# A transformer layer on one core: the last two gate projections together, the last up projection between the first two pairs of score matmuls

## The reference

```
xn   = layernorm(x)
q, k, v = bitnet_linear(xn, q_weight), ...   # sign of the weights, a scale for each output
scores  = q @ k.T / sqrt(16)                 # 32 heads of 16; 8 key and value heads, each for 4 query heads
attn = softmax(scores) @ v
hidden = silu(xn @ gate_w.T) * (xn @ up_w.T) # 1792 wide, ternary weights with a scale
out  = x + bitnet_linear(attn, o_weight) + hidden @ down_w.T
```

## Time and profile before

| | us |
|---|---|
| median of 3 runs | 501.98 |
| the profiled execution | 501.71 |
| its span | 500.0 |
| PE busy | 480.1 |
| DVE busy | 415.7 |
| ACT busy | 348.1 |
| last unit F27: first matmul | 148.45 |
| first score matmul | 152.01 |

### The profile page before, as it was taken

How to read it: one execution, slowest core, us unless ns; L and a number is a source line. 1 busy time by engine, 2 the same in 40 slices (tenths; PEclk the granted TensorE clock), 3 DMA queues, 4 the chain that set the end, 5 groups by cost and what they waited for, 6 DMA issues and landing times.

```text
span 500.0 us, 10314 instructions
## 1 busy us (share of the span) xinstructions
PE 480.1 (96%) x4171; PEld 163.6 (33%) x4171; DVE 415.7 (83%) x487; ACT 348.1 (70%) x640; POOL 101.7 (20%) x154
## 2 busy tenths in 40 slices
PE   1899999999998999999999999999999999999996
PEld 0564444433332222222222222222222233333442
DVE  7879868676777999999999999999999955223986
ACT  1943543352228999999999999999999978774000
POOL 4212334534424011011011011001101213241021
PEclk9999999999998999999999999999999999999999
DMA  8853783642103812212212312222221133453321
GB/s 263 266 109 84 165 163 41 182 93 24 22 0 40 152 25 42 64 25 43 64 24 44 65 39 47 43 55 34 42 64 25 15 108 94 102 156 86 105 83 45
DMA packets 64424, 39.28 MB, mean 79 GB/s; under 512 B 39729, under 2 KB 53937, under 8 KB 64377
## 3 DMA queue, kind: packets, MB, share of 16 engines
q1 hardware_dynamic: 55352, 27.59, 22.6%
q0 software_dynamic: 8304, 10.95, 11.8%
q10 hardware_dynamic: 720, 0.08, 0.1%
HBM read 33.37 MB, written 10.48 MB: 88 GB/s over the span
## 4 chain that ended last, share of the span: by engine, by line
PE 93%; DVE 3%; ACT 2%; DMA 1%; issue 1%; SPq 0%; ACTq 0%; DVEq 0%
PE ps L1309 28%; PE ps L1144 19%; PE ps L1247 14%; PE ps L1153 11%; PE ps L1217 5%; PE ps L1204 5%; PE ps L1125 4%; PE ps L1339 3%; PE ps L1278 2%; ACT room L718 2%; DMA hlo<-x 1%; DVE stats L777 1%; DVE room L799 1%; PE ps L1117 1%; DVE room L804 0%
## 5 line engine op out<-in xcount | busy, mean ns | idle before, releaser
L853 DVE TENSOR_REDUCE nmx<-ps 128x1 f32<-128x1024 f32 x248 | 283.2, 1216 | 13.4 <-PE ps L1153 13.2
L718 ACT ACTIVATE room<-ps 128x512 f32<-128x512 f32 x512 | 271.1, 598 | 20.5 <-PE ps L1278 11.5
L1309 PE MATMUL ps<-room,vcur 128*32 128x256 f32 (+1 forms) x1880 | 159.8, 412 | 0.3 <-ACT room L718 0.3
L1153 PE MATMUL ps<-kA,qst 48*128 48x512 f16 x496 | 139.3, 384 | 0.0
L1247 PE MATMUL ps<-qst,kB 50*128 50x512 f16 x432 | 134.8, 384 | 1.3 <-ACT room L718 1.3
L1144 PE MATMUL ps<-room,wf 128*128 128x512 f16 x448 | 100.6, 379 | 0.0
L1309 PEld LDWEIGHTS ps<-room,vcur 128*32 128x32 f32 x1880 | 37.2, 108 | 95.0 <-issue 52.1
L699 ACT ACTIVATE room<-ps,gsc 128x512 f32<-128x512 f32 x28 | 19.2, 686 | 62.4 <-PE ps L1144 62.4
L1144 PEld LDWEIGHTS ps<-room,wf 128*128 128x128 f16 x448 | 42.4, 98 | 55.1 <-issue 7.2
L1247 PEld LDWEIGHTS ps<-qst,kB 50*128 50x128 f16 x432 | 28.3, 93 | 97.0 <-ACT room L718 84.6
L562 POOL TENSOR_SCALAR mxs<-mxs 16x128 f32<-16x128 f32 x16 | 8.3, 520 | 214.8 <-DMA mxs<-m_scratch 214.6
(11 more groups left out here) (137 smaller groups left out, 316.9 us busy)
## 6 DMA issues: line engine op xcount, KB each, us to landing
qst<-q_scratch SPq DMA_DIRECT2D x32, 192.0 KB, 3.6
o_scratch<-osb SPq DMA_DIRECT2D x16, 256.0 KB, 2.5
q_scratch<-parts SPq DMA_DIRECT2D x12, 256.0 KB
hlo<-x SPq DMA_DIRECT2D x8, 256.0 KB, 5.3
parts<-x POOLq DMA_DIRECT2D x8, 256.0 KB, 3.7
wf<-gate POOLq DMA_DIRECT2D x14, 128.0 KB, 3.8
wf<-up POOLq DMA_DIRECT2D x14, 128.0 KB, 5.9
wd<-down POOLq DMA_DIRECT2D x1, 1792.0 KB, 13.9
```

The costliest lines, as they stand in the source:

```text
L718: nc.scalar.activation(probs[:, s % 2, r, :], ps[:, bank_of(step, i), :], ACT.Exp, scale=gam_reg[par][r]).then_inc(scores_free, 1)
L853: nc.vector.tensor_reduce(nmx[:, hf, idx:idx + 1], bank_pair(idx % 2), AX.X, ALU.max, negate=True).then_inc(rows_free, 1)
L1153: return nc.tensor.matmul(ps[:, 2 * (idx % 2) + b, :], qst[low:low + KROWS, par, hf, head, qt * P:(qt + 1) * P], kA[low:low + KROWS, par, ...
L1309: mm = nc.tensor.matmul(ps[32 * r:32 * r + 32, value_bank(step_ // TT), of], vcur[:, par, key_tile(r, j), :], probs[:, s % 2, r, of], star ...
```

## The change

Three edits at the passage. On PE, G27 follows G26 at once, then A30 and A31, then U26; U27 is issued in the middle of the first step, behind score 1. On ACT, the rounding of F26 goes behind the first two exponentials, and the wait for U27 stands before the third. The first two exponentials (heads 0 and 2, `EARLY`) are written into the weight buffers 2 and 3 of `wf`, whose last readers are U23 and the units before it, and `times_values` reads them there. `dve_order` and `act_order` are unchanged.

```diff
-                "A17 F20 ... A28 A29 F26 A30 A31 F27 ")
+                "A17 F20 ... A28 A29 G26 G27 A30 A31 U26 ")
...
+    EARLY = ROUND[:REP // 2]
...
+        early_probs = wf[:, :, :, :].rearrange("p a z n -> p (a z n)").bitcast(F32)[:, 2 * HALF:].rearrange("p (r n) -> p r n", r=2)
...
+        def probs_of(step, r):
+
+            if step == 0 and r in EARLY:
+                return early_probs[:, EARLY.index(r), :]
+            return probs[:, step % 2, r, :]
...
-                    if n >= 1:
+                    if 1 <= n < FU - 1:
                         hidden_high(n - 1)
...
+            exps(0, 0, False, range(REP // 2))
+            hidden_high(FU - 2)
             act.wait_ge(up_ready, FU)
-            exps(0, 0, False)
+            exps(0, 0, False, range(REP // 2, REP))
             hidden_high(FU - 1)
...
-                    if opening and i == 0:
+                    if s == 0 and i == 0:
                         pe.wait_ge(gt_ready, FU)
+                    if s == 0 and i == 2:
+                        pe.wait_ge(h_ready, FU - 1)
...
-            pe.wait_ge(h_ready, FU - 1)
             pe.wait_ge(kones_ready, 2)
-            scores(0, 0, opening=True)
+            scores(0, 0, range(REP // 2))
+            feed_forward(FU - 1, 1)
+            scores(0, 0, range(REP // 2, REP))
```

More of the change, by code:

```diff
@@ L60, in layer_kernel @@
                 "F8 A3 A4 F9 A5 F10 F11 F12 A6 A7 F13 F14 A8 A9 F15 A10 A11 F16 A12 A13 F17 A14 A15 F18 A16 S1 F19 "
-                "A17 F20 A18 A19 F21 A20 A21 F22 A22 A23 F23 A24 A25 F24 A26 A27 F25 A28 A29 F26 A30 A31 F27 ")
+                "A17 F20 A18 A19 F21 A20 A21 F22 A22 A23 F23 A24 A25 F24 A26 A27 F25 A28 A29 G26 G27 A30 A31 U26 ")
     dve_order = ("M0 M1 J0 M2 J1 M3 H0 M4 R0 M5 N0 N1 M6 M7 L0 H1 N2 R1 N3 N4 L1 N5 L2 N6 N7 L3 L4 L5 L6 L7 J2 S0 Z0 "
@@ L79, in layer_kernel @@
     assert pe_order.index(("F", SPLIT_AT)) > pe_order.index(("A", UNITS - 1))
-    assert [n for kind, n in pe_order if kind in "FU"] == list(range(FU))
+    assert [n for kind, n in pe_order if kind in "FU"] == list(range(FU - 1))
     assert dve_order.index(("A", SUM_AT - 1)) < dve_order.index(("S", 1)) < dve_order.index(("A", SUM_AT))
@@ L707, in load_scale, with exps @@
                 act.reg_load(gam_reg[par][r], gam_words[0:1, bass.ds(g * REP + r, 1)])
-            def exps(gp, s, last):
+            def exps(gp, s, last, entries=range(REP)):
                 gp_, par, hf, j = at(gp, s)
@@ L715, in exps @@
                 act.wait_ge(probs_free, step + 1)
-                for i, r in enumerate(ROUND):
+                for i in entries:
+                    r = ROUND[i]
                     act.wait_ge(scores_ready, step * REP + i + 1)
-                    nc.scalar.activation(probs[:, s % 2, r, :], ps[:, bank_of(step, i), :], ACT.Exp,
+                    nc.scalar.activation(probs_of(step, r), ps[:, bank_of(step, i), :], ACT.Exp,
                                          scale=gam_reg[par][r]).then_inc(scores_free, 1)
@@ L1220, in down_proj, with scores @@
                     mm.then_inc(down_ready, 1)
-            def scores(gp, s, opening=False):
+            def scores(gp, s, entries=range(REP)):
                 gp_, par, hf, j = at(gp, s)
                 block_ = gp * 4 + s // TT
-                if j == 0:
+                if j == 0 and 0 in entries:
                     pe.wait_ge(q_loaded[par][hf], 32 * (gp_ + 1))
@@ L1258, in scores @@
                             half_rows(1 - par, hf, idx, half).then_inc(rows_ready, 1)
-                    if i % 2 == 1 and not opening:
+                    if i % 2 == 1 and s > 0:
                         times_values(gp, s - 1, i // 2, 2)
@@ L1309, in times_values @@
                     mm = nc.tensor.matmul(ps[32 * r:32 * r + 32, value_bank(step_ // TT), of], vcur[:, par, key_tile(r, j), :],
-                                          probs[:, s % 2, r, of], start=(j == 0 and part == 0),
+                                          probs_of(step_, r)[:, of], start=(j == 0 and part == 0),
                                           stop=(j == TT - 1 and part == cut - 1))
```

## The result

| | before | changed |
|---|---|---|
| median of 22 runs, us | 502.2 | 504.9 |
| lowest and highest, us | 500.27, 505.42 | 503.19, 507.44 |
| profiled execution's span, us | 500.0 | 501.5 |

The ratio is 1.0057, 95% interval 1.0042 to 1.0072: the change makes the kernel 2.1 to 3.6 us slower. In a second comparison (12 and 33 runs, medians 505.42 and 502.65) it is 1.0062, 1.0031 to 1.0092. Three executions that lie far above the others of their kernel (766 us in e5, 1140 us in e10, 510 us in e6) count in no ratio.

What follows compares the result with a forecast made beforehand. The prediction took DVE's row maxima from R5 on to bound the kernel. It added 0.78 us for R5's later reduction and 1.3 for the halved clock to 501.71, giving 503.8 us, range 501.9 to 504.9 (8 in 10).

Steps and rivals of the forecast that it cites:

- What bounds the kernel: Attention from R5 on: DVE's row maxima set the pace, 1.1315 us each; moving R5's reduction moves the end equally.
- G26, G27, ACT: Passage before attention: G27 waits 0.10 us, score 0 issued at 150.36, Exp table loaded before it.
- ACT's old wait: PE's 1.28 us idle for the late Exp table load and exponentials; forecast to go, worth nothing by itself.
- The new wait: PE before R0: idle 1.72 us until DVE reduces A30, which stands behind F26's product; R0 issued at 152.47.
- Rival "faster": Wait at R0 does not bind, A30 being reduced before score 0 is issued: -1.33, 500.4 us; chance 0.07.
- slow stretch: PE at half clock after idle time; before, 156.2 to 159.5 us, costing DVE 1.50 us; one forecast after the change.
- The price of the wait and the order without the clock: R5's reduction starts at 161.23 against 160.45 if DVE runs R0 to R5 without a hole: +0.78 us.
- The clock: Idle time before U27 or R2 can halve PE's clock; price taken as 1.3 us, between 0 and 1.73.
- Same wait, clock stays at 1.00: Rival: PE waits at R0 but no slow stretch follows, 502.5 us; chance 0.24.
- The base: Whole kernel before: the profiled execution's 501.71 us, without adding the 0.27 by which the median of runs lay above.
- the two terms of the sum: Added to the kernel before: +0.78 us for R5's later reduction and +1.3 us for the halved clock.
- Two slow stretches in one run: Rival: half clock once in U27 and once behind R2, 4.0 us more, 505.7 us; chance 0.10.

Runs made afterwards that it cites:

- e5: Changed kernel with DVE reducing A30 and A31 ahead of F26's product and R0 ahead of F27's; medians 500.20, 501.03, 500.48 us; ratios 0.9934, 0.998, 0.9962.
- e10: Kernel before with one row maximum done twice on DVE in step 20, the extra result unused; 502.41 us against 502.24.
- e6: Changed kernel with U27 straight behind U26, ahead of all scores, and A30 and A31 reduced ahead of F26's product on DVE; 503.72 us, ratio 1.0015.
- e1: Changed kernel with A30 and A31 reduced ahead of F26's product on DVE; 503.07 us against 503.05, ratio 1.0001.
- e4: Kernel before with six unused matmuls filling PE's idle time in front of score 3; 502.11 us against 503.05, ratio 0.9993.
- e7: Changed kernel with unused matmuls filling PE's idle times, 8 in front of R0 and 5 in front of R2; 503.43 us against 502.65, ratio 0.9999.
- e3: Changed kernel with U27 straight behind U26, ahead of all scores; 505.59 us, ratio 1.0038.

## Why the prediction was right or wrong

*What bounds the kernel: held.* R5's reduction moved by +2.62 and the last row maximum by +2.55 us. e10 tests it: of 1.13 us put on DVE, 1.06 come out. The end of one execution does not follow as exactly, since the tail behind the last row maximum differs from run to run (last section).

*G26, G27, ACT: held.* Score 0 comes 6.12 us after G26 (6.01 expected), the Exp table is loaded before it, and ACT's old wait is gone and worth nothing.

*The new wait: held.* PE idles 1.72 us in front of R0, released by DVE's reduction, as worked out. In the second profile, where U27 runs at full clock, R0's reduction comes 11.41 us after G26 (155.57 - 144.35 = 11.22 expected); of the 0.2 about half arises at G27 and half in front of U27. That its absolute times fit even better (152.47 for R0 on PE) is luck, as G26 starts 0.1 earlier there. The edit that removes the wait's cause, e1, removes it. Rival "faster" fell on the order of DVE; e1's stretch is 1.21 us shorter than before (1.33 expected), but that is the slow stretch missing, and beside e4 the edits on PE and ACT give nothing.

*The price of the wait and the order without the clock: nearly.* + 0.78 forecast; e7 has + 0.95 against the profile of before. Its R0 is 0.2 late, as is that of the second profile of the changed kernel, where nothing fills the wait.

*The clock: the mechanism held, its size nearly.* I took 1.3 us between 0 and 1.73. Against e7 the two profiles of the changed kernel lose 1.60 (over U27) and 1.14 (behind R3), mean 1.37; so far the sum is + 2.3 against the profile of before, not + 2.1. The close mean is partly luck: 1.3 stood for a single case, and two different ones came. I also took the slow stretch as given on both sides; in fact 44 of 114 runs of the kernel before have none. "Same wait, clock stays at 1.00", 502.5 us, did not come in either profile, and the eight runs in which it came by their mean clock took 504.9 us. The traces again disagree with the rule of the Trainium skill, page "TensorE: Matmul & The Clock Gate", section "Why this matters for your kernels", by which these idle times are too short to take the clock down: it fell with no uninterrupted idle time over 1.72 us in the one profile and over 1.28 us just before the fall in the other.

*The base was mis-sized.* The step that failed, and put the range wrong, is the last one of the sum: "The median of the runs shown, 501.98, is 0.27 above that execution; I don't add it." The kernel before is 502.2 us over 22 runs and up to 503.05 in the other comparisons, 0.5 and more above the 501.71 of its profiled execution. The end of my range lay 504.9 - 501.71 = 3.2 us above the base; on 502.2 it would have been 505.4. With the base put right, 2.3 on 502.2 is 504.5; 504.905 was measured, just past the end of my range (504.9). So of the 1.1 us between 503.8 and the measured time the base is 0.5, the two terms of the sum are 0.2, and 0.4 is unexplained. As a change, 2.7 us were measured (2.1 to 3.6) against 2.1. What is left, about 0.4 us, lies within that interval. Two slow stretches in one run may be a part of it (four runs of the first comparison had a clock under 0.995 and 503.9 to 506.9 us, three of the second 507 to 510 us), but I have no profile of such a run.

*What stays open.* In the first comparison 6 runs of the changed kernel with a clock of 0.998 or more were no faster (504.86 us) than 12 with 0.995 to 0.997 (504.93). Such runs of the kernel before take 501.5 us, so without a slow stretch the change costs 3.4 us in times, where the profiles of e7 and e4 give 2.28. No run of the changed kernel without a slow stretch was profiled, so where this further 1.1 us lies is not shown. It does not touch the cause: with the order of e1 on DVE such runs take 501.6 us.

## What to carry to other kernels

When work is reordered on one engine, put the hand-written order of every engine that frees its buffers beside it: here a matmul order was changed and the reduction that frees the banks stayed behind a product that now comes later. Removing a wait gains only what the engine that sets the pace of the next stage gains; count the time at which that engine starts its unbroken run, not the idle time that disappears. Take the base of a forecast from the median of many runs and not from the one that was profiled. Short idle times of TensorE have a second price, half the clock for a while after them, that comes in some runs only.

## What the runs showed that I had not expected

- The same idle time can be followed by a slow stretch or not: e1 and the second profile of the changed kernel both have 1.28 us in front of R2; the clock stayed at 1.00 in e1's profile and fell to 0.50 in the other. And of the two profiles of the changed kernel, both with 1.7 us in front of R0, only the first has a clock of 0.50 over U27.
- Two exchanges in DVE's order (e5) made the changed kernel faster than the kernel before; the second puts a reduction into an idle time of DVE.
- Executions differ by 2 to 3 us outside the passage. G26 starts between 143.82 and 146.16 us in these profiles; the latest, e3, also has the later landing of the first tiles of x (4.80 us in the kernel before, 7.10 in e3, by the chain of waits). From the last row maximum to the end of the span it is 101.4 us in the changed kernel and 103.4 in its second profile, where PE waits 1.20 us for ACT at 459.80 and DVE waits longer for the reciprocals to come back from memory. A change of 1 us is seen in the passage's own rows, not in the medians.
